# Block products by a seven-product scheme in an attention kernel: scores of two tiles by 1024 keys, and weights turned by block transposes and an exchange in SBUF

## The reference, cut

```python
h = jnp.maximum(_layernorm(x, axis=-1), 0.0)          # x: 4096 x 256
q = h @ Wq.T + bq;  k = h @ Wk.T + bk;  v = h @ Wv.T + bv
a = q @ k.T * scale + adj + adj                       # adj: 4096 x 4096, scale = 1/16
x = x + jax.nn.softmax(a, axis=-1) @ v
```

## Time and profile before

| | us |
|---|---|
| median of 3 runs (lowest, highest) | 759.6 (759.54, 761.32) |
| span of the profiled execution | 759.2 |
| TensorE busy | 728.7 (96%) |
| ScalarE busy | 552.8 (73%) |
| VectorE busy | 467.2 (62%) |
| GpSimd busy | 68.7 (9%) |
| transposing DMAs, share of the 16 DMA engines | 54.6% |
| loads and stores, share of the 16 DMA engines | 36.1% |

### The profile page before, as it was taken

The page is one execution under the profiler, slowest core; times in us unless marked ns, Lnnn a source line. Parts: engine busy times, 40 slices in busy tenths (PEclk is TensorE's granted clock), DMA queues, the critical chain, the costliest instruction groups (busy, mean ns, idle before and its releaser), DMA issues.

```text
span 759.2 us, 14115 instructions
## 1 busy us (share of the span) xinstructions
PE 728.7 (96%) x3964; PEld 394.1 (52%) x3964; DVE 467.2 (62%) x1237; ACT 552.8 (73%) x1011; POOL 68.7 (9%) x120
## 2 busy tenths in 40 slices
PE   5599979999999999999999999999999999999996
PEld 4376434555555555555555555555555555555553
DVE  4597555655666666666655666666666666666663
ACT  4387577787777777777877777777777877777763
POOL 2011000010011001000010010000000000000000
PEclk9699999999999999999999999999999999999999
DMA  7600099999999999999999999999999999999966
GB/s 251 241 1 1 1 156 209 191 224 215 205 213 209 202 216 206 203 213 206 206 211 206 214 205 207 214 209 205 206 209 210 202 209 213 206 211 210 209 123 125
DMA packets 298607, 143.74 MB, mean 189 GB/s; under 512 B 273376, under 2 KB 281952, under 8 KB 298592
## 3 DMA queue, kind: packets, MB, share of 16 engines
q10 hardware_dynamic: 270336, 67.14, 54.6%
q1 hardware_dynamic: 28256, 76.43, 36.1%
HBM read 72.22 MB, written 4.19 MB: 101 GB/s over the span
## 4 chain that ended last, share of the span: by engine, by line
PE 91%; DMA 3%; ACT 2%; issue 2%; ACTq 1%; DVE 1%; SPq 0%; POOL 0%; DVEq 0%
PE bank L686 90%; DMA wT<-w_split 2%; ACTq L472 1%; PE bank L720 1%; ACT rows L449 1%; ACT w_split L459 1%; DMA bk_sb<-in_L_gnn_bk 0%; DVE hT_lo L519 0%; ACT rows L433 0%; PE bank L710 0%; SPq L249 0%; DVE wvT_lo L591 0%; DVE tops L563 0%; DVE rows L625 0%; ACT m_hi L414 0%
## 5 line engine op out<-in xcount | busy, mean ns | idle before, releaser
L686 PE MATMUL bank<-v_sb,wT 128*128 128x512 f16 (+1 forms) x2048 | 375.2, 327 | 8.0 <-DMA wT<-w_split 8.0
L686 PE MATMUL bank<-hT_hi,g_tile 128*128 128x512 f16 x1024 | 344.4, 379 | 1.4 <-issue 1.4
L619 DVE TENSOR_TENSOR w_split<-rows,w_split 128x512 f16<-128x512 f32 x256 | 184.2, 720 | 242.3 <-PE bank L686 198.3
L686 PEld LDWEIGHTS bank<-v_sb,wT 128*128 128x128 f16 x2048 | 199.6, 98 | 170.1 <-DMA wT<-w_split 13.4
L449 ACT ACTIVATE rows<-rows,exp_bias,exp_scale 128x512 f32<-128x512 f32 x256 | 206.2, 806 | 82.1 <-DVE exp_bias L649 75.9
L433 ACT ACTIVATE rows<-rows,adj_scale 128x1024 f32<-128x1024 f32 x128 | 146.7, 1148 | 68.6 <-issue 57.7
L686 PE MATMUL bank<-hT_lo,g_tile 128*128 128x512 f16 x512 | 194.3, 379 | 0.0
L625 DVE CUSTOM_DVE_ANT_0 rows<-bank,rows 128x512 f32<-128x512 f32 x256 | 174.7, 683 | 5.7 <-PE bank L686 5.7
L686 PEld LDWEIGHTS bank<-hT_hi,g_tile 128*128 128x128 f16 x1024 | 100.4, 98 | 122.9 <-issue 2.2
L459 ACT CAST w_split<-rows 128x512 f16<-128x512 f32 x256 | 154.7, 604 | 11.8 <-DMA wT<-w_split 11.1
L358 POOL TENSOR_TENSOR x_bias<-x_sb,bv_row 128x256 f32<-128x256 f32 x32 | 25.6, 801 | 577.8 <-DMA out_y<-y 577.8
(11 more groups left out here) (73 smaller groups left out, 265.6 us busy)
## 6 DMA issues: line engine op xcount, KB each, us to landing
rows<-in_adj SPq DMA_DIRECT2D x128, 512.0 KB, 4.5
x_sb<-in_x SPq DMA_DIRECT2D x8, 512.0 KB, 4.4
wT<-w_split ACTq DMA_TRANSPOSE x256, 3.8
out_y<-y SPq DMA_DIRECT2D x32, 128.0 KB, 1.8
wq_sb<-in_L_gnn_Wq SPq DMA_DIRECT2D x1, 256.0 KB, 3.7
wk_sb<-in_L_gnn_Wk SPq DMA_DIRECT2D x1, 256.0 KB, 3.8
wv_sb<-in_L_gnn_Wv SPq DMA_DIRECT2D x1, 256.0 KB, 5.3
bv_row<-in_L_gnn_bv SPq DMA_DIRECT2D x1, 128.0 KB, 5.4
```

The lines of the kernel that those rows point to most:

```text
L619: nc.vector.tensor_tensor(w[:, 1, :], rows[at // CHUNKS % 2][:, cols], w[:, 0, :], ALU.subtract).then_inc(split_lo, 1)
L686: return nc.tensor.matmul(out_ap, stationary, moving, start=first, stop=last)
```

## The change

**Scores.** The unit of scoring is now a period: two tiles (256 queries) by 1024 keys (two chunks) by 256 features, seen as a product of 2 x 2 blocks of 128 by 128 and 128 by 512. Seven block products with sums of blocks take the place of eight (the Strassen scheme in Winograd's form). There are 64 periods, 4 for each of 16 pairs of tiles. The blocks of the keys and their sums (`T1` to `T4`) are made once: GpSimd adds (`key_sums`), ScalarE and VectorE split into the 7 slots of `top`. The blocks of the queries and their sums (`S1` to `S4`) are made for each pair (`query_sums`, `high_query`, `query_low`) from `g`, which goes through a scratch tensor in HBM. The seven products share four PSUM banks: `t_ps` is added to by products 1, 6, 7 and 4 in turn, and VectorE reads it after each (`scores_11`, `scores_12`, `scores_22`, `finish_21`); products 2, 5 and 3 go to `u_ps` and `w_ps`.

**Weights.** A unit is a tile by 2048 keys, 4 chunks, numbered m = 4u to 4u + 3. After the exponential VectorE transposes each chunk in blocks of 32 by 32 (`turn`); ScalarE and GpSimd split it into `w_split`, high and low halves interleaved (`high`, `low`); SyncE issues four plain DMAs a chunk from SBUF to SBUF (`exchange`), each 32 partitions by 8 pieces of 256 bytes, that bring the blocks to their partitions in `wT`. The rows of `v` are permuted in the same way (`move_v`). `weigh` of unit u runs in period u + 6, in four parts, with three matmuls of 256 columns for each 128 keys, and its first part waits for all four chunks. Its stationary operand is read from `wT` with a step of four elements.

**Order.** All loops are unrolled. `turn`, `exchange` and the rest are placed by period; the first periods also hold the projections (`fill`), and the reduction of the maxima over partitions is done with a transpose and a small matmul. `g_pair` and `xy` are loaded for each pair.

```diff
-                    act.dma_start_transpose(
-                        wT[:, at % W_RING],
-                        w_split[:, at % SPLIT_RING].rearrange("p s k -> p (s k)")
-                        ).then_inc(transposed[at % 2], 16)
...
-            def score(pair, j):
-                c = j % CHUNKS
...
-                wait(pe, summed, chunk_no(pair, j) - SCORE_BANKS + 1)
-                keys = slice(c * CH, (c + 1) * CH)
-                g = g_tile[b]
-                three_products(score_ps[j % SCORE_BANKS][:],
-                               [(g[:, 0, k, :], g[:, 1, k, :], hT_hi[:, k, keys],
-                                 hT_lo[:, k, keys]) for k in range(DC)]).then_inc(scored, 1)
...
-            def weigh(pair, j):
-                c, b, at = j % CHUNKS, j // CHUNKS % 2, j % W_RING
-                pe.wait_ge(transposed[j % 2], pair * (16 * UNROLL // 2) + 16 * (j // 2 + 1))
-                for k in range(KT):
-                    kt = c * KT + k
-                    matmul(o_ps[b][:], wT[:, at, k, :],
-                           v_sb[:, kt].rearrange("p s d -> p (s d)"), kt == 0, False)
-                    last = matmul(o_ps[b][:, 0:D], wT[:, at, KT + k, :],
-                                  v_sb[:, kt, 0, :], False, kt == CHUNKS * KT - 1)
-                last.then_inc(weighed, 1)
```

SyncE's new functions and its period:

```diff
+            def store(t):
+                slot = t % XY
+                sp.wait_ge(y_done, t + 1)
+                sp.dma_start(out[t * P:(t + 1) * P, :], xy[:, slot, :]).then_inc(stored[slot], 16)
...
+            def exchange(m):
+                u, k = m // 4, m % 4
+                sp.wait_ge(split_lo, m + 1)
+                wait(sp, weighed, 4 * (u - 1))
+                for i in range(P // Q):
+                    sp.dma_start(wT[k * Q:(k + 1) * Q, u % 2, :, i * Q:(i + 1) * Q
+                                    ].rearrange("p n q b s -> p n (q b s)"),
+                                 w_split[i * Q:(i + 1) * Q, k].rearrange("p n q b s -> p n (q b s)")
+                                 ).then_inc(moved[k], 16)
+                if m % 2 == 1:
+                    p, half, t = unit_parts(u)
+                    r = 2 * (QUADS * p + 2 * half + k // 2) + t + ROW_UNITS
+                    if r < 2 * PERIODS:
+                        load_rows(r)
...
+            def period(n):
+                p = n // QUADS
...
+                if n % QUADS == 0 and p + 1 < PAIRS:
+                    load_g(p + 1)
+                for m in (4 * (n - EXP_LAG) - 3, 4 * (n - EXP_LAG) - 2):
+                    if 0 <= m < 4 * PERIODS:
+                        exchange(m)
+                if n % QUADS in (1, 2) and p >= 2:
+                    store(2 * (p - 2) + n % QUADS - 1)
+                for m in (4 * (n - EXP_LAG) - 1, 4 * (n - EXP_LAG)):
+                    if 0 <= m < 4 * PERIODS:
+                        exchange(m)
+                if n % QUADS == 3 and 1 <= p and p + 1 < PAIRS:
+                    load_xy(2 * p + 2)
+                    load_xy(2 * p + 3)
```

Splitting on GpSimd and ScalarE:

```diff
+            def low(m):
+                if 0 <= m < 4 * PERIODS:
+                    pool.wait_ge(split_hi, m + 1)
+                    nc.gpsimd.tensor_tensor(split_part(m, 1), turned_blocks(chunk_row(m)),
+                                            split_part(m, 0), ALU.subtract
+                                            ).then_inc(split_lo, 1)
...
+                wait(act, moved[m % 4], 64 * (m // 4))
+                nc.scalar.copy(split_part(m, 0), turned_blocks(chunk_row(m))).then_inc(split_hi, 1)
```

VectorE, the passes over PSUM, the block transpose and the output; then its period:

```diff
+            def scores_11(n):
+                dve.wait_ge(row_loaded(n, 0), row_loads(n, 0))
+                dve.wait_ge(t_done, 4 * n + 1)
+                part = score_part(n, 0, 0)
+                nc.vector.scalar_tensor_tensor(part, part, adj_scale[:], t_ps[n % 2][:], ALU.mult,
+                                               ALU.add).then_inc(t_read, 1)
...
+            def add_with_max(n, t, part, ps):
+                k = 2 * (n % QUADS) + part
+                row = score_part(n, t, part)
+                p = n // QUADS
+                return nc.vector.tensor_tensor_reduce(
+                    out=row, in0=ps[:], in1=row, scale=1.0, scalar=-3.0e38, op0=ALU.add,
+                    op1=ALU.max, accum_out=chunk_max[:, p % 2, t, k:k + 1])
...
+            def finish_21(n):
+                dve.wait_ge(adj_scaled, n + 1)
+                dve.wait_ge(t_done, 4 * n + 4)
+                add_with_max(n, 1, 0, t_ps[n % 2]).then_inc(t_read, 1)
+            def turn(m):
+                if 0 <= m < 4 * PERIODS:
+                    dve.wait_ge(exped, m + 1)
+                    nc.vector.transpose(chunk_row(m), chunk_row(m)).then_inc(turned, 1)
...
+            def finish(tile):
+                t = tile % 2
+                y = xy[:, tile % XY, :]
+                dve.wait_ge(sum_step, 3 * tile + 3)
+                dve.wait_ge(weighed, 4 * (tile_units(tile) + 1))
+                dve.wait_ge(xb_done, tile + 1)
+                nc.vector.scalar_tensor_tensor(y, o_ps[t][:, 0:D], out_scale[:, t:t + 1], y, ALU.mult,
+                                               ALU.add).then_inc(y_done, 1)
...
+            def period(n):
...
+                if scoring:
+                    scores_11(n)
+                if 1 <= n <= PERIODS:
+                    finish_12(n - 1)
+                if n % QUADS == 0 and 1 <= p <= PAIRS:
+                    bias(2 * p - 2)
+                turn(4 * u - 1)
...
+                if scoring:
+                    scores_12(n)
+                    finish_11(n)
+                if n % QUADS == 0 and 1 <= p <= PAIRS:
+                    bias(2 * p - 1)
...
+                turn(4 * u)
...
+                if scoring:
+                    scores_22(n)
+                    finish_22(n)
...
+                turn(4 * u + 1)
...
+                if scoring:
+                    finish_21(n)
...
+                if n % QUADS == 0 and p >= 2:
+                    sums(2 * p - 4)
+                if n % QUADS == 1 and p >= 2:
+                    finish(2 * p - 4)
+                    sums(2 * p - 3)
+                if n % QUADS == 2 and p >= 2:
+                    finish(2 * p - 3)
+                if n % QUADS in (2, 3) and p < PAIRS:
+                    row_bias(2 * p + n % QUADS - 2)
```

TensorE, a block product, the weighing and the period:

```diff
+            def product(ps, n, a, b, first):
+                p, q = n // QUADS, n % QUADS
+                if p == 0:
+                    pe.wait_ge(top_lo, 7 * q + b + 1)
+                a_hi, a_lo = a_op[:, p % 2, 0, a], a_op[:, p % 2, 1, a]
+                b_hi, b_lo = top[:, b, q, 0], top[:, b, q, 1]
+                for k, (s, mv) in enumerate(((a_hi, b_hi), (a_hi, b_lo), (a_lo, b_hi))):
+                    last = nc.tensor.matmul(ps[:], s, mv, start=first and k == 0, stop=k == 2,
+                                            skip_group_check=True)
+                return last
...
+            def product_4(n):
+                pe.wait_ge(t_read, 4 * n + 3)
+                product(t_ps[n % 2], n, A22, T4, False).then_inc(t_done, 1)
...
+            def weigh(u, part):
+                p, half, t = unit_parts(u)
+                if part == 0:
+                    for c in range(HALF_CHUNKS):
+                        pe.wait_ge(moved[c], 64 * (u + 1))
...
+                w = wT[:, u % 2]
+                for k in range(4):
+                    block = 4 * part + k
+                    kt = half * BLOCKS + block
+                    run, b2 = block // RUN, block % RUN
+                    w_hi, w_lo = w[:, run, :, b2, 0], w[:, run, :, b2, 1]
+                    matmul(o_ps[t][:, 0:D], w_hi, v_sb[:, kt, 0], half == 0 and block == 0, False)
+                    matmul(o_ps[t][:, 0:D], w_hi, v_sb[:, kt, 1], False, False)
+                    last = matmul(o_ps[t][:, 0:D], w_lo, v_sb[:, kt, 0], False,
+                                  half == 1 and block == BLOCKS - 1)
+                last.then_inc(weighed, 1)
...
+            def period(n):
+                scoring = n < PERIODS
+                if scoring:
+                    product_1(n)
+                if 1 <= n <= PERIODS:
+                    product_3(n - 1)
+                fill(n, 0)
+                if scoring:
+                    product_6(n)
+                    product_2(n)
+                fill(n, 1)
+                if scoring:
+                    product_7(n)
+                    product_5(n)
+                fill(n, 2)
+                if scoring:
+                    product_4(n)
+                fill(n, 3)
```

## The result

The change makes the kernel slower: **1110.3 us** (median, 1106.5 to 1115.9) against 759.6 (756.3 to 761.3) for the kernel before on the same chip, a ratio of 1.462 with a 95% interval of 1.456 to 1.468. The profiled execution has a span of 1104.8 us. The prediction had the side right (slower), but 797 us and a range of 740 to 870; the time lies 240 us above its upper end.

What follows compares the result with a forecast made beforehand. The prediction took TensorE to bound the kernel. Start 41, fill 74, 58 periods of 9.77 us (567) and drain 46 made 728; 28 store waits of 2.5 us (69) made 797 us, range 740 to 870.

Steps and rivals of the forecast that it cites:

- The pace of TensorE: Steady periods: 21 matmuls of 512 columns and 48 of 256 take 9.77 us, against 10.36 before.
- rival 4: Weighing: stationary operand with a step of 8 bytes loads slowly, 12.1 us a period, 930 us in all; chance 0.05.
- SyncE's issue of 0.42 us: SyncE's queue, each period: 19.25 DMA issues at 0.42 us take 8.1 us, range 6.4 to 9.0.
- all five lie under 9.77: Steady periods: VectorE, ScalarE, GpSimd, SyncE and the DMA engines each need less than TensorE's 9.77 us.
- Rival 3: Steady periods: a queue other than TensorE's sets the pace, 11.0 us a period, 867 us in all; chance 0.10.
- The store in the middle: Exchange queue: a store waiting for `y_done` delays chunk 3, so TensorE waits 2.5 us 28 times, 69 us.
- rival 2: Exchange after the store: same wait with a landing of 3.8 us, 28 x 4.4, 851 us in all; chance 0.09.
- The prediction's own sign of failure: TensorE's waits on the exchange: forecast wrong if they are absent or lie in all four periods of a pair.
- The cast: ScalarE's passes, the cast into `w_split` among them, taken at 604 ns each, five a period.
- The landing: End of an exchange DMA: 1.8 us taken from a 128 KB store, 3.8 as the far value.
- The start and the fill: Before steady periods: first projection at about 20 us, first score at 41, then periods 0 to 5 in 74.
- The drain: Last six periods, without scores: SyncE's queue and weighing share a loop, 7.1 us a period, 46 us with the last output.

Runs made afterwards that it cites:

- e_pair: Kernel after with one exchange DMA a chunk (no exchange between partitions), store behind the fourth exchange, next pair's query operands earlier: 838.5 us, 892.6 without the last edit.
- e_fill: Kernel after with exchange issues split between SyncE and ScalarE, store moved, 2048-byte pieces, four groups normalised between key casts: 984.7 us, 993.3 without the last edit.
- e_store: Kernel after with only the store moved behind the period's fourth exchange DMA: 1080.5 us, against 1110.3 for the kernel after.

## Why the prediction was right on the side and wrong on the size

**The pace of TensorE: right.** 0.109 us a weighing matmul and 9.77 us a period were forecast; groups of 12 in 1.31 us and periods of 9.84 were measured where nothing else was late. The strided weight loads (rival 4) cost nothing that shows, and splitting the wide matmul cost 3 us in the kernel before. With three disturbances removed (issues, store, boundary), 58 periods took 601.5 us (`e_pair`, 187.8 to 789.3), 10.37 each. In after itself the lower clock adds 1.4 us a period, for which the sum had no term, since it had no waits that could bring it.

**The step that failed: SyncE's issue of 0.42 us.** The prediction took the loads at the kernel's start for the nearest row and had 0.47 as its upper end. The exchange's issue is 0.59 us at least and 0.65 from one to the next. That makes 16 x 0.65 = 10.4 us of exchange alone, 12.2 with the loads and a store, above TensorE's 9.77 before any wait; the forecast had 8.1. It fits the whole stretch: SyncE's waits for `xy` and for the low halves are 67.3 + 61.4 = 128.7 us, 2.2 a period, so that at least 12.4 of 14.61 us go to issues. The sentence "all five lie under 9.77" is where the sum went wrong (for the DMA engines it held only at the low end of their 9.4 to 16.8). Rival 3 named the class (a queue other than TensorE's) but priced only the DMA engines and VectorE, at 1.2 us a period, and neither bound: from 190 to 1037 us the DMA engines' share was 0.72, and VectorE was busy for 485 of 847 us. The measured excess is 14.61 - 9.77 = 4.8, with the store's wait in it. With the number of issues cut to a quarter, 166 us went.

**The store in the middle: right mechanism, other size.** The chain through `y`, the store and four issues is in the trace, and TensorE's wait behind it is 3.4 us where 2.5 were forecast: from `y` to the weighing 4.7 us passed in place of 13.53 - 9.92 = 3.6. Yet the price of the store's place, forecast as 69 us, is 52 when the queue has room and 30 in the kernel as it is, because the queue is late without it too. SyncE's waits do name VectorE's `xy` 28 times, as forecast, but with 2.4 us each in place of 4, since SyncE comes to the store late. (Two of the sums are slightly off: by their terms the lower end of the wait is 2.1 and not 2.0, and rival 2 has 4.5 and not 4.4. It changes nothing.) The prediction's own sign of failure, waits on the exchange in all four periods of a pair, is what the trace has.

**No term for the boundary of a pair.** The sum put the operands of the next pair under GpSimd's 7.3 us and asked only whether that fits in a period. It fits, and yet TensorE waits for the last low half. Moving those low halves and their casts earlier gave 54 us.

**The cast: wrong by a factor of two, harmless.** 1342 ns, not 604; 8 to 11 us in two tests. GpSimd's low half (1.36 for 1.41) and the transpose (0.71 for 0.61 to 0.70) were well sized. **The landing** is 2.9 us for 1.8, inside the range taken.

**The start and the fill.** The first projection came at 20.3 us, as forecast (20). The first score came 11 us and the first weighing 75 us late. The sum added engine work, stage by stage, and had 74 us for the fill; from 52.1 to 190 us TensorE is busy for 80.3 and waits for 57.6. The longest wait, 12.8 us, is the first weighing's, on its own exchange, for which the sum had no term. The others are on chains through several queues, with `DVE top`, `ACT w_split` and `DVE vn` as releasers, 9.4 us the longest. `e_fill` moved the layernorm of four groups and took 8.5 us off. The first weighing is nearly as late in `e_pair` (187.8, with 9.9 us on the exchange), so the number of issues has little part in it. The rest of the excess has only the trace's word.

**The drain.** 46 us forecast, 67 after, 45 in `e_pair`: with a quarter of the issues the estimate holds, which points to SyncE's queue again.

Adding up from after, by the runs: 166 for the issues, 52 for the store, 54 for the boundary, which leads from 1110 to the 838 of `e_pair`. That kernel leaves out the exchange between partitions, and each step holds what the clock gave back with the waits. Its span, 834.8, is 107 us over the forecast's 728 without the store: 73 at the start, 35 for 0.6 us a period. TensorE's saving of 0.59 us a period (10.36 to 9.77, 38 us in all) is real, and about a tenth of what was lost around it.

## What to carry to other kernels

Price a DMA issue by the same kind of DMA, and multiply by the count, before asking about bytes: sixteen small SBUF-to-SBUF copies a period cost more in the issuing queue than in transfer, and an issue of a known DMA can cost more in a new queue (the loads here, 333 and then 600 ns). For each queue, a sum under the period is not enough; ask at which place in the queue each instruction stands and who waits for it. When a change has several parts, try them alone: the smallest one here (maxima on TensorE) was the only one that paid.

## What the runs showed of the hardware

- The issue of an exchange DMA held the issuing queue for 0.58 to 0.61 us (medians; 0.63 on ScalarE's queue) in every shape tried: 32 partitions by 8 pieces of 256 bytes, 32 by one of 2048, 128 by 8 of 256. SyncE and ScalarE issued side by side at that price, and ScalarE computed meanwhile; on GpSimd it was the engine's time. What stood before it mattered to other DMAs: a store from SBUF to HBM had 0.35 us when the queue had been idle and 0.60 right behind an exchange (`e_store`), and the load of 128x1024 had 0.33 in the kernel before and 0.60 after. In after no exchange had less than 0.585, in either place.
- ScalarE's cast of 512 elements to float16 took 1342 ns with a step of 8 bytes within the chunk's output, 1100 with runs of 16 elements and reads 128 bytes apart, 614 when both were contiguous. For GpSimd's subtraction these were 1359, 1481 and 1163.
- Weight loads with a step of 8 bytes held the pace of 0.109 us. With 64 bytes their mean was 147 ns (119 in after), and twelve matmuls still took 1.31 us at the full clock.
- The granted clock fell with TensorE's waits: 0.876 over the kernel after, 1.00 from 190 to 790 us in `e_pair`, where it had few. At the lower of the two levels (1.2 and 2.4 GHz) six matmuls of 512 columns took 2.56 us in place of 1.30.
